# Latent queries and keys of a cross-attention: where the mean squares are scaled, when the roots of the norms are taken, and where a side chain of last rows stands

## The reference

```python
q = (ln @ Wq).reshape(b, m, h, d).transpose(0, 2, 1, 3)     # ln = layernorm(latents)
kv = jnp.concatenate([xn @ Wkv, ln @ Wkv], axis=1)          # xn = layernorm(context)
...
qn = rmsnorm(q, qn_g) * scale                               # over d = 64, for each of h = 16 heads
kn = rmsnorm(k, kn_g)
```

## Time and profile before

| | us |
|---|---|
| median of 3 runs | 2583.28 |
| lowest and highest run | 2577.11, 2585.13 |
| the profiled execution | 2586.15 |
| span of its trace, first to last instruction | 2583.9 |

### The profile page before, as it was taken

The page is one execution under the profiler, slowest core; times in us unless marked ns, Lnnn a source line. Parts: engine busy times, 40 slices in busy tenths (PEclk is TensorE's granted clock), DMA queues, the critical chain, the costliest instruction groups (busy, mean ns, idle before and its releaser), DMA issues. The chain is left out here.

```text
span 2583.9 us, 64446 instructions
## 1 busy us (share of the span) xinstructions
PE 2436.0 (94%) x24562; PEld 1900.6 (74%) x24577; DVE 1692.7 (66%) x3969; ACT 1281.2 (50%) x2972; POOL 1469.5 (57%) x1669
## 2 busy tenths in 40 slices
PE   6999999999999999999888997799999999998997
PEld 3457888878787878787566586688888888886665
DVE  5777868686868677774576733566655665654665
ACT  3665656565656565654442232354445444543443
POOL 6986757676767675755762254576446644331333
PEclk9999999999999999999898998899999999999998
DMA  5242211111111121211005188433224423210001
GB/s 186 107 157 61 61 41 41 41 42 40 46 36 48 33 50 31 51 27 25 20 4 190 54 266 263 152 110 103 69 75 99 95 67 79 72 46 15 4 4 35
DMA packets 224819, 190.05 MB, mean 74 GB/s; under 512 B 89217, under 2 KB 212674, under 8 KB 224514
## 3 DMA queue, kind: packets, MB, share of 16 engines
q1 hardware_dynamic: 208994, 153.92, 20.2%
q0 software_dynamic: 9216, 27.28, 4.4%
q10 hardware_dynamic: 6304, 4.72, 0.6%
HBM read 151.53 MB, written 34.31 MB: 72 GB/s over the span
## 5 line engine op out<-in xcount | busy, mean ns | idle before, releaser
L295 POOL TENSOR_TENSOR rk<-ss,neg_half 128x32 f32<-128x32 f32 x64 | 348.7, 5448 | 248.2 <-DVE ss L277 248.2
L1847 PE MATMUL banks<-rowsT,qk 128*128 128x257 f32 x1024 | 244.8, 382 | 3.8 <-issue 3.8
L328 ACT ACTIVATE ksq<-kT 128x512 f32<-128x512 f32 x256 | 161.1, 629 | 161.2 <-DVE kT L271 161.2
L271 DVE COPY kT<-banks 128x512 f32<-128x512 f32 x256 | 176.9, 692 | 60.5 <-PE banks L382 56.4
L382 PE MATMUL banks<-x_hi,wk_hi 128*128 128x256 f32 x1024 | 213.6, 289 | 1.1 <-DVE kT L271 1.0
L1847 PEld LDWEIGHTS banks<-rowsT,qk 128*128 128x128 f32 x1024 | 190.6, 191 | 30.9 <-issue 4.1
L382 PE MATMUL banks<-x_hi,wk_lo 128*128 128x256 f32 x1024 | 207.0, 284 | 0.0
L382 PE MATMUL banks<-x_lo,wk_hi 128*128 128x256 f32 x1024 | 205.7, 282 | 0.5 <-DVE x_lo L263 0.5
L1254 ACT ACTIVATE score<-score,ntop 128x289 f32<-128x289 f32 x256 | 135.4, 530 | 115.6 <-DVE ntop L1118 115.4
L1685 POOL CAST r_hi<-diff 128x512 fp32r<-128x512 f32 x64 | 42.8, 669 | 248.3 <-PE banks L1873 244.8
L1656 POOL DMA_INDIRECT parts<-scratch_expert,address x128 | 131.2, 1025 | 91.8 <-DVE residual L1550 45.9
(11 more groups left out here) (369 smaller groups left out, 6528.6 us busy)
## 6 DMA issues: line engine op xcount, KB each, us to landing
rowsT<-in_ctxT SPq DMA_DIRECT2D x64, 257.0 KB
wgu<-in_expert_gu SPq DMA_DIRECT2D x64, 256.0 KB
rows<-in_ctx SPq DMA_DIRECT2D x64, 256.0 KB
raw<-in_ctx SPq DMA_DIRECT2D x61, 256.0 KB
scratch_qT<-qT SPq DMA_DIRECT2D x16, 512.0 KB, 2.6
scratch_kT<-kT SPq DMA_DIRECT2D x16, 512.0 KB, 3.0
q<-scratch_qT SPq DMA_DIRECT2D x64, 128.0 KB
kT<-scratch_kT SPq DMA_DIRECT2D x64, 128.0 KB
```

Source lines behind the costliest of these rows:

```text
L271: nc.vector.tensor_copy(m.kT[:, k, 2 * i:2 * i + 2, 0:ROWS], banks[i % 2].rearrange("p (a r) -> p a r", a=2)).then_inc(s.kT, 1)
L295: nc.gpsimd.tensor_tensor(m.rk[:], m.ss[:], kit.neg_half[:, 0:KF * H], ALU.pow).then_inc(s.rk, 1)
L328: nc.scalar.activation(m.ksq[:, 2 * i:2 * i + 2, :], m.kT[:, k, 2 * i:2 * i + 2, 0:ROWS], ACT.Square).then_inc(s.ksq, 1)
L1847: mm = nc.tensor.matmul(score[h][:, c - h * HALF, 0:CTX], m.qk[:, f, j, c * BT:(c + 1) * BT, :].rearrange("p h q -> p (h q)"), m.rowsT[:, ...
```

## The change

- The scaling of the mean squares (times 1/64, with a floor) is taken off POOL and done by DVE, one instruction behind each sum. POOL keeps the powers alone.
- Tiles 4 to 15 are split into MIDDLE (4 to 7) and LAST (8 to 15). The statistics of LAST are taken by DVE between steps 1 and 2, their roots by POOL after steps 1 and 2, and used by DVE in step 5.
- The wait for eight loads becomes three: `norm_in` for gain, offset and identity before the first tile (48), `w_in` for the query weights and the small gains before the first product (80), and `gain` before the first scaled queries.
- The split of the weights moves to steps 5 to 8, the chain of the last rows four steps later (`LATER = 4`), `norm_rows` from steps 4 and 7 to behind steps 10 and 11, and the bias is added to two tiles a step in steps 6 to 11.

```diff
-    FIRST, REST = range(NT // XP), range(NT // XP, NT)
+    FIRST, MIDDLE, LAST = range(NT // XP), range(NT // XP, NT // 2), range(NT // 2, NT)
+    LATER = 4
...
-                    sp.dma_start(sb[:], src.partition_broadcast(P)).then_inc(s.w_in, 16)
-                sp.dma_start(kit.ident[:], d.ident).then_inc(s.w_in, 16)
+                    sp.dma_start(sb[:], src.partition_broadcast(P)).then_inc(s.norm_in, 16)
+                sp.dma_start(kit.ident[:], d.ident).then_inc(s.norm_in, 16)
...
-                dve.wait_ge(s.w_in, 128)
-                nc.vector.tensor_copy(kit.ident16[:], kit.ident[:]).then_inc(s.ident16, 1)
-                nc.vector.scalar_tensor_tensor(m.gain[:, 2:3], m.gain[:, 0:1], DH ** -0.5, m.gain[:, 1:2], ALU.mult, ALU.mult).then_inc(s.gain, 1)
                 roots(FIRST, 1)
-                dve.wait_ge(s.gain, 1)
+                dve.wait_ge(s.norm_in, 48)
...
                     nc.vector.tensor_reduce(m.ssq[:, k, :], m.qsq[:].rearrange("p (h e) -> p h e", h=H), AX.X, ALU.add).then_inc(s.qss, 1)
+                    dve.wait_ge(s.qss, n + 1)
+                    nc.vector.tensor_scalar(m.rq[:, k, :], m.ssq[:, k, :], 1.0 / DH, 1e-16, ALU.mult, ALU.max).then_inc(s.rq_scaled, 1)
...
                     if n == 1:
-                        roots(REST, 2)
+                        roots(MIDDLE, 2)
+                    if n == 5:
+                        roots(LAST, 3)
...
-                    if n >= 2:
-                        biased(n - 2)
+                    if 6 <= n < 12:
+                        biased(2 * n - 12)
+                        biased(2 * n - 11)
...
                 def inverse_norms(n, k):
-                    hold(pool, s.qss, n + 1, s.passed)
-                    inv_root(nc, pool, kit.neg_half[:, 0:H], m.rq[:, k, :], m.ssq[:, k, :], 1.0 / DH, 1e-16, ALU.max, s.rq_scaled, n + 1, s.rq)
+                    pool.wait_ge(s.rq_scaled, n + 1)
+                    nc.gpsimd.tensor_tensor(m.rq[:, k, :], m.rq[:, k, :], kit.neg_half[:, 0:H], ALU.pow).then_inc(s.rq, 1)
...
-                pe.wait_ge(s.w_in, 128)
-                pe.wait_ge(s.ident16, 1)
+                pe.wait_ge(s.norm_in, 48)
...
                 rows_T(0, 0)
                 rows_T(1, 1)
+                pe.wait_ge(s.w_in, 80)
                 queries(0, 0)
```

More of the change, by code:

```diff
@@ L447, in latent_queries @@
         m = named({**m._asdict(), "high": fm.kT[:, 0].rearrange("p a r -> p (a r)")[:, 0:FC * INNER].rearrange("p (f n) -> p f n", f=FC)})
-        s = kit.sems("lat", "w_in wk_in last_in valid_in half set ident16 stats aggr eps r1 r1sq var2 r2 r gain cent ln_ready hi lo lnT_ps lnT k_ps k_sq k_copied kss "
+        s = kit.sems("lat", "norm_in w_in wk_in last_in valid_in half set ident16 stats aggr eps r1 r1sq var2 r2 r gain cent ln_ready hi lo lnT_ps lnT k_ps k_sq k_copied kss "
                      "q_ps q_sq q_copied qss rq_scaled rq rk_scaled rk qh kh qT_ps qT_low qT_high kT_ps kT last_cent passed lastn last_hi last3 lastT_ps lastT kl_ps kl_sq "
@@ L627, in _ @@
                 key_sums(0, 0)
+                dve.wait_ge(s.gain, 1)
                 queries(0, 0)
                 step(0)
-                variances(REST, 2)
+                variances(MIDDLE, 2)
+                step(1)
+                moments(LAST)
+                f.norm_stats(0, 0, 1)
+                step(2)
+                variances(LAST, 3)
                 dve.wait_ge(s.last_in, 48)
                 row_stats(nc, dve, [m.last[:]], m.stats[0:B, NT:NT + 1, :], m.mvl, s.stats, s.aggr, NT)
-                f.norm_stats(0, 0, 1)
@@ L641, in _ @@
-                step(2)
+                nc.vector.scalar_tensor_tensor(m.lastn[:], m.last[:], m.mvl[:, 0, 0:1], m.g_x[:], ALU.subtract, ALU.mult).then_inc(s.last_cent, 1)
+                dve.wait_ge(s.last_cent, 1)
+                dve.wait_ge(s.r2, 4)
+                nc.vector.scalar_tensor_tensor(m.lastn[:], m.lastn[:], m.rl[:, 0:1], m.b_x[:], ALU.mult, ALU.add).then_inc(s.lastn, 1)
+                step(7)
                 nc.vector.tensor_tensor(cross.mk.wk_lo[:], m.wk[:], m.high, ALU.subtract).then_inc(s.split, 1)
+                step(8)
@@ L657, in _ @@
                 scaled(m.high[0:B, 1, :], m.rkl[:], s.klh)
-                step(6)
+                step(10)
                 dve.wait_ge(s.klT_ps, 1)
                 nc.vector.tensor_copy(kit.last_kT[:].rearrange("p a b -> p (a b)"), kit.psum(1)).then_inc(s.klT, 1)
-                step(7)
+                f.norm_rows(0, 0, 0)
+                step(11)
                 f.norm_rows(1, 1, 1)
-                for n in range(8, NT - 2):
-                    step(n)
+                step(12)
+                step(13)
                 n, u = NT - 2, NT // 2 - 1
@@ L755, in _ @@
                     nc.gpsimd.tensor_scalar(m.mask[:, at:at + rows.stop - rows.start], m.valid[:, rows], 1.0, MASKED, ALU.subtract, ALU.mult).then_inc(s.masked, 1)
-                for n in range(7, NT - 2):
+                step(6)
+                step(7)
+                step(8)
+                hold(pool, s.kl_ss, 1, s.passed)
+                inv_root(nc, pool, kit.neg_half[0:B, 0:H], m.rkl[:], m.ssl[:], 1.0 / DH, 1e-16, ALU.max, s.rkl_scaled, 1, s.rkl)
+                step(9)
+                hold(pool, s.last_hi, 1, s.passed)
+                nc.gpsimd.tensor_tensor(m.last3[:, 2, :], m.lastn[:], m.last3[:, 0, :].bitcast(F32), ALU.subtract).then_inc(s.last3, 1)
+                for n in range(10, NT - 2):
                     step(n)
```

73 lines of the change are left out of this document (36 added, 37 removed).

## The result

| | before | after |
|---|---|---|
| median of the runs side by side, us | 2580.0 (5 runs) | 2567.18 (5 runs) |
| lowest and highest run | 2577.09, 2585.13 | 2560.49, 2573.8 |
| ratio, with its 95% interval | 1 | 0.9945 (0.993 to 0.9959) |
| span of the profiled execution | 2583.9 | 2567.8 |

The kernel became faster by 0.55%, some 14 us (10.6 to 18 by the interval). The forecast was 2578.8 with a range from 2572.5, and no measurable change as the likeliest case. It was wrong, on the side of rival 2.

What follows compares the result with a forecast made beforehand. PE, busy 94% of the span, was taken as the bound, with gains only from its waits, mainly for DVE's scaled keys. The terms summed to -4.45 us, from 2583.28 to 2578.8, range 2572.5 to 2586.5.

Steps and rivals of the forecast that it cites:

- rival 2: Whole stage: POOL was all, DVE keeps pace, PE fills every step from 1 on; 2572.3 us, chance 0.12.
- the price of a key root: POOL in steps 0 and 1: scaling moved away, but key power slowed by DVE's scaling to 3.70; saves 0.6 us each.
- Steps 0 and 1: First two tile steps: shorter POOL chain and smaller first root save 2.9 us; bounds -3.9 and -1.5.
- step 2: PE's stall before the key transposes stays at 3.1 to 3.2 because of DVE's 8-tile statistics: -0.9 us; bounds -4.1, +0.5.
- step 3: Stall before the key transposes goes, with DVE relieved and POOL ahead: -1.4 us; bounds -1.5 and 0.
- Head: Ahead of step 0: without the wait for small gains everything comes earlier, -2.05 us; bounds -2.05 and 0.
- Rival 1: Head's gain stays in ACT's queue, load `bo` ending at 20.65 as before; 2580.9 us, chance 0.22.
- the backlog in order of issue: Head: DMA loads share one backlog served as issued, so ACT's hold moves earlier and all 2.05 us arrive.
- The clock window that was to follow the stall: After step 2's stall PE again runs at a clock of about 0.5; such windows cost 1.7 us each.
- Steps 4 to 13: Up to tile 15's query product: small stalls from POOL's and DVE's moved work and the moved chain, +3.1 us.
- Rival 3: Slower: DVE takes POOL's place in every step, 13 steps lose 0.33 each plus clock windows; 2586.6 us, chance 0.12.

Runs made afterwards that it cites:

- `s_scale`: Kernel before with only the scaling of the mean squares moved from POOL to DVE; ratio 0.9959 to before, last query product starting at 164.32 us.
- `x_gap`: Kernel after with three added POOL waits between query power and key power, so DVE's scaling of the queries starts first; ratio 0.9974 to before.
- `s_head`: Kernel before with only the head changed: separate semaphore for the norm's inputs, wide wait moved behind the first two norms; ratio 1.0 to before.
- `after_2`: Kernel after, unchanged, run and profiled again; ratio 0.9948 to before, last query product starting at 159.20 us.
- `b_all`: Kernel after with the last rows' key transposes one step later and the last 8 tiles' statistics in two portions of 4; ratio 0.9936 to before.
- `b_all_2`: `b_all` unchanged, run again beside the kernel after; ratio 0.9922 to before.
- `u_late`: Kernel after with weight split, last rows' chain and bias additions back at their early steps; ratio 0.9969 to before.

## Why the prediction was wrong

**The step that failed** is the price of a key root in "Steps 0 and 1": "the power that now meets DVE's scaling takes 3.70 [...] So 1.31 + 0.08 + 2.92 = 4.31 becomes 3.70: 0.6." The 3.70 was read from a row of before in which the key power began 0.30 us after DVE's scaling. But there POOL's own scaling stands between the two powers, and it is this that lets DVE start first. The change removes exactly that instruction. Nothing is left between the powers, POOL starts the second one 0.07 to 0.12 us ahead of DVE, and it takes 2.91 (tile 0, rows of `s_scale` and after). A key root saves 1.4, the value that the prediction named and set aside. The steps' terms that were built on it came out too small: by 0.9 us in steps 0 and 1, by 2.2 in step 2, by 1.1 in step 3. The kernel `x_gap` shows it from the other side: with the order turned round the key power takes 3.71, steps 0 and 1 win 2.83 (predicted 2.9), step 2 has a stall of 3.31 (predicted 3.1 to 3.2), and the mark is at 166.59 (predicted 167.5, or 167.84 by the terms of the sum; 168.3 with the clock falling in step 11 as it did in after). The prediction describes that kernel rather than the one that ran, though not exactly: from the end of the query power a key root takes 4.08 us there, with the added idle time, where the prediction had 3.70.

**Two sums that do not come out as written.** Step 2's terms (4.8 + 2.82 + 0.4 + 0.9 + 1.2 + 0.25 + 1.2) add up to 11.6 and not to 11.1, and PE got to the key transposes at 8.13 in before, not at 7.95 (59.49 less the wait of 4.13, less 47.23). Put right, the stall would have been 3.4 and the term -0.7, further from the result; `x_gap` had 3.31. Rival 2's terms (15.8 - 0.9 - 0.8, less one stretch of 1.7 at the lower clock, and the head's 2.05) come to 14.4 and not to 11, which is 2568.8 and not 2572.3. The range's lower end was taken from that 11.

**Point by point.**

- Head, -2.05: measured -1.72 and, between the second profiles, -2.43. Rival 1 is refuted: the load `bo` was issued at 13.76 instead of 15.78, held ACT for 4.41, and its issue ended at 18.17 instead of 20.65. What the prediction did not see is that this gain needs the portions; alone it was lost in step 0 (`s_head`). Nor is the backlog in order of issue, as the prediction read it: in after the last quarter of the rows, issued at 8.2, landed 14.0 us later, while ACT's queue, whose first load was issued at 12.57, moved 0.54 MB from 16.6 to 19.4 us.
- Steps 0 and 1, -2.9: -3.77. The bound of -3.9 held it.
- Step 2, -0.9: -3.13. The working was right in form, and its first input was wrong: scaled queries at 3.6 to 4.8 us into the step, where they end at 3.1. The bound of -4.1 held it. The clock window that was to follow the stall did not come; the window of after from 51 to 55 us (granted clock: the first number behind POOL's):

```profile
51.00:55.00 4.00, 3.52 (x14) 2.06 (x15) 3.93 (x7) 1.71 (x3) 4.00 (x2) 1.00 0.52 207
```

- Step 3, -1.4: -2.48, since with the clock at its upper level all the excess of 2.48 went.
- Steps 4 to 13, +3.1: +1.11, and -0.57 between the second profiles, where the clock fell in before and not in after. Small stalls were added one by one (+1.1 in step 4, +0.6, +1.4) from POOL's and DVE's work in single steps. In after steps 4 to 6 have none; step 7 costs 0.97. I read it so, that without the scalings POOL has time to spare in every step and makes up a burst in one before PE feels it. This is 2 of the 5.8 us that the sum was off at the mark. `x_gap` has +1.02 without the fall of the clock, +2.7 with it, in steps 6 and 7 (9.49 and 11.07) and none in step 4: with the key root at the predicted price or above, the size is nearly the predicted one, and the place is not.
- Rival 2, "POOL was all", at 2572.3, is nearest to what happened: PE fills every step from 0 to 6 but step 2. It was given 0.12 because the order puts statistics ahead of the keys; they cost 1.61, not 3.1.
- Rival 3 is refuted: DVE's scalings take 0.15 to 0.2 as expected, and no step behind the ninth is over 9.3 without a reason of its own.

**What was not seen at all** is that the terms are no sum. The mark shows 9.99 for all four parts; one at a time they give +0.9, -7.7 and +2.8 (head, scaling, chain), and without the scaling the other three give 0.4 (the clock fell behind the wait for the last keys in before and after and in none of these four, so 1.7 us of each difference to before is that). The scaling is worth so much because POOL had almost nothing to spare. From step 8 on a step takes 9.10 us with and without it; what it wins lies in steps 0 to 3, where POOL was busy for 9.75 of 10.57, 10.99 of 11.49, 13.18 of 14.02 and 10.66 of 11.58 us in before. Late in the stage its margin can be read. Windows of one step late in the stage, of before, `s_head` and `s_scale` (POOL's busy time is the fifth):

```profile
135.59:144.69 9.10, 9.06 (x36) 4.89 (x35) 6.74 (x9) 6.04 (x10) 8.77 (x6) 1.00 0.37 144
```

```profile
144.93:154.25 9.32, 9.28 (x37) 4.89 (x36) 7.20 (x9) 5.99 (x10) 8.98 (x6) 1.00 0.37 142
```

```profile
127.92:137.02 9.10, 9.06 (x36) 4.90 (x35) 6.92 (x11) 6.06 (x10) 7.53 (x4) 1.00 0.37 144
```

In before POOL is busy for 8.77 of 9.10 us, so once behind it can win back some 0.3 us a step, an estimate from these two numbers. In `s_head` it fell into an order in which both of its scalings meet DVE's, and then POOL sets the step: 9.31 us for the last five. With the scaling gone it has 1.6 us a step to spare. POOL's busy time could be read in the profile of before; the prediction priced only the steps with a visible wait.

Open remains why the first pair of spans differs by 6.1 us behind the mark. Executions of one kernel differ there by more (after and `after_2` by 12.5 us; `b_all` and `b_all_2` have marks within 0.13 us and spans of 2575.0 and 2561.7; both pairs on two chips), so no part of it is put down to the change.

## What to carry to other kernels

When a change removes an instruction, do not price its neighbours by rows in which that instruction still stands: ask who can start first once it is gone. Here a tenth of a us decided whether a power took 2.9 us or 3.7. Before a stall is priced on its own, compare the busy time per step of the engine behind it with the step itself; an engine with 0.3 us to spare in 9.1 hardly makes up for a delay. And parts of one edit should be forecast together where one removes what another would run into, as the portions of the statistics did for the head and the moved chain for the portions. And where the clock falls behind a wait in one execution and not in the next, profile both kernels twice before a difference of 1.7 us is given to an edit.

## What the runs showed of the hardware

- When a POOL power (128x16) and DVE's two-input scaling (128x1024) overlap, the power pays if it began second: 3.28 to 3.82 us in all 113 such pairs in the stage's fourteen traces, against 2.89 to 3.11 in 116 of the 130 in which it began first (3.15 to 3.52 in the rest). The surplus is a little less than what is left of DVE's instruction: 0.8 in `x_gap`, where 0.95 was left. DVE's scaling took 1.21 to 1.27 in either order, so it did not pay for being second. Beside another POOL instruction, `lo` (128x256), it did take 1.74 (`s_head`, at 151.30). The Trainium skill ("SBUF — State Buffer", Who interferes with whom) names the contention for a read interface; the prediction drew from it that the key power had to pay. The same section says that issue order decides who blocks, which the prediction passed over. The rows agree for the power and not for DVE.
- Two POOL instructions of which the second waits for an engine that has long signalled follow each other with no gap at all (the first ends at 26.85 in the records and the second starts at 26.81), while DVE starts on the first one's result at 26.93.
- A power of 4, 8 and 16 columns took 1.01, 1.64 and 2.90 us in after; the prediction's slope had 1.65 for 8.
- A wait of 1.65 us ahead of PE was followed by the lower clock in one execution of the kernel after (0.66 in the window) and not in another (1.00), nor in `s_scale` and `u_late`, which have the same wait.
- The last quarter of the rows, issued by SP at 8.2 us, landed 10.7 to 11.6 us later in the four traces without the head, where ACT's first load of weights was issued at 14.1 to 14.6, and 13.8 to 15.7 us later in the ten with it, where that load was issued at 12.5 to 12.6.
